# Layer norm statistics inside a state-space scan: ScalarE running sums in the place of VectorE batch-norm instructions

## The reference

```
def _layernorm(x, axis=-1, eps=1e-05):
    m = jnp.mean(x, axis=axis, keepdims=True)
    v = jnp.var(x, axis=axis, keepdims=True)
    return (x - m) / jnp.sqrt(v + eps)
...
    h = _layernorm(x, axis=-1) * (1 + ca) + sa
    x = x + ga * _L1_attn_ref(h, L1_attn_W_in, L1_attn_conv_w, L1_attn_conv_b, L1_attn_W_xproj, L1_attn_log_A, L1_attn_D_param, L1_attn_W_out)
    h = _layernorm(x, axis=-1) * (1 + cb) + sb
    x = x + gb * _L1_ffn_ref(h, L1_ffn_router_w, L1_ffn_w1, L1_ffn_w2, L1_ffn_bias)
```

## Time and profile before

| | us |
|---|---|
| median of 3 runs | 1818.52 (1814.84 to 1818.67) |
| the profiled execution, device time | 1820.8 |
| its span | 1819.1 |
| busy: PE, POOL, DVE, ACT over the whole span | 1502.0, 1346.1, 1152.2, 797.8 |
| stretch 1330 to 1602 (272 us): DVE busy | 258.09 |
| the same stretch: ACT, POOL, PE busy | 164.75, 194.84, 155.26 |
| mean granted TensorE clock, of full speed | 0.907 |

### The profile page before, as it was taken

One profiled execution on the slowest core, in us unless ns is written; L12 is line 12 of the kernel. 1 busy time (PEld: TensorE's weight loads), 2 busy tenths in 40 slices (PEclk: granted clock), 3 DMA queues, 4 the chain that ended last, 5 costly groups with the idle time before them and its releaser, 6 DMA issues. The chain is left out here.

```text
span 1819.1 us, 26796 instructions
## 1 busy us (share of the span) xinstructions
PE 1502.0 (83%) x8699; PEld 1034.9 (57%) x8699; DVE 1152.2 (63%) x2579; ACT 797.8 (44%) x1379; POOL 1346.1 (74%) x1154
## 2 busy tenths in 40 slices
PE   5899999999999999999999998988965664357970
PEld 3455556766556755656755657877833232136960
DVE  6866766566676575676566504755589998952224
ACT  2245444345444344444344453444486775323320
POOL 5587988788898698898788783536576657658376
PEclk7699999999999999999999998999977876667995
DMA  6333334231222122131131103024485555424333
GB/s 177 70 89 82 71 71 83 70 70 42 65 58 48 48 56 50 36 70 36 47 70 36 36 13 86 23 72 114 109 199 126 141 133 132 108 69 146 99 86 87
DMA packets 125761, 146.65 MB, mean 81 GB/s; under 512 B 15784, under 2 KB 84796, under 8 KB 125624
## 3 DMA queue, kind: packets, MB, share of 16 engines
q1 hardware_dynamic: 118456, 130.60, 29.3%
q0 software_dynamic: 7168, 14.34, 2.9%
HBM read 65.24 MB, written 29.42 MB: 52 GB/s over the span
## 5 line engine op out<-in xcount | busy, mean ns | idle before, releaser
L838 DVE CUSTOM_DVE_ANT_0 ring<-ring,mask 128x128 f32<-128x128 f32 (+7 forms) x512 | 383.8, 769 | 186.3 <-PE ring L700 185.9
L924 ACT ACTIVATE prob<-ring 128x512 f32<-128x512 f32 x576 | 315.2, 597 | 298.1 <-PE ring L715 294.5
L978 POOL TENSOR_TENSOR acc<-acc,prob 128x512 f32<-128x512 f32 x272 | 353.1, 1298 | 73.0 <-ACT prob L924 49.4
L731 PE MATMUL ps_o<-prob,v 128*64 128x256 f32 x2304 | 282.5, 387 | 3.9 <-issue 3.8
L700 PE MATMUL ring<-k,x 128*128 128x512 f32 (+3 forms) x768 | 252.0, 408 | 35.8 <-ACT prob L924 22.1
L714 PE MATMUL ring<-x,k 128*128 128x512 f32 x576 | 258.1, 448 | 24.6 <-DVE neg_m L838 15.4
L715 PE MATMUL ring<-x,k 128*128 128x512 f32 x576 | 229.4, 398 | 0.0
L700 PEld LDWEIGHTS ring<-k,x 128*128 128x128 f32 x768 | 137.3, 198 | 144.5 <-ACT prob L924 50.9
L731 PEld LDWEIGHTS ps_o<-prob,v 128*64 128x64 f32 x2304 | 154.6, 137 | 106.5 <-issue 39.6
L2929 POOL TENSOR_TENSOR m_hc<-m_st,m_crep 128x1024 f32<-128x1024 f32 x64 | 150.8, 2357 | 71.7 <-DVE m_st L2672 64.0
L975 POOL TENSOR_TENSOR acc<-prob 128x512 f32<-128x512 f32 x144 | 184.4, 1281 | 8.5 <-ACT prob L924 7.2
(11 more groups left out here) (414 smaller groups left out, 2816.1 us busy)
## 6 DMA issues: line engine op xcount, KB each, us to landing
x<-other SPq DMA_DIRECT2D x256, 128.0 KB, 2.3
m_x_rep<-u_mem SPq DMA_DIRECT2D x64, 512.0 KB, 4.7
x<-rot SPq DMA_DIRECT2D x128, 128.0 KB, 2.3
sorted_in<-zeros SPq DMA_DIRECT2D x3, 1548.0 KB, 11.9
e_sorted<-sorted_in SPq DMA_DIRECT2D x18, 258.0 KB, 3.7
sorted_out<-e_hid SPq DMA_DIRECT2D x18, 256.0 KB, 2.2
slots_in<-zeros SPq DMA_DIRECT2D x2, 2048.0 KB, 8.7
slots_out<-wo SPq DMA_DIRECT2D x16, 256.0 KB, 2.4
```

What stands on the lines that cost most here:

```text
L731: mm = e.matmul(ps_o[s * D:(s + 1) * D, qb % 2 * 2 * P:(qb % 2 + 1) * 2 * P], v[g % 2][:, kb, :], prob[i % NPROB][:, s * 2 * P:(s + 1) * 2 ...
L838: e.tensor_tensor_reduce(ps, ps, mask_1[:, SEQ - n:SEQ], 1.0, -3.0 * NEG, ALU.add, ALU.min, neg_m[g % 2][:, c, h, qb % QPC:qb % QPC + 1]). ...
L924: e.activation(prob[i % NPROB][:, :], banks(("s2",) + key, BANK), ACT.Exp, scale=-1.0).then_inc(s2_exp.sem, 1)
L978: e.tensor_tensor(total[:, :], total[:, :], tile[:, :], ALU.add).then_inc(summed.sem, 1)
```

## The change

For `join` and for `out` of batches 0 to 2 (ten halves in all), the statistics are made by ScalarE:

- the copy of a PSUM bank, one instruction of 128x512, becomes four of 128x128, each with a running sum over its row into `row_sum`;
- at the plan positions of `sums` and `stats`, ACT makes `row_mid` = -sum/128 (128x4) and then, behind a semaphore wait, four 128x128 squares of (x + row_mid), each with a running sum into `row_sq`; the squares themselves go to a scratch tile;
- at `rstd1` and `rstd3`, ACT makes the mean and the variance (two 128x8 copies into `mv`), and takes the logarithm with the scale 1/128 from `row_sq`.

DVE loses the ten calls of `row_stats`. The last batch's `out` keeps its statistics on DVE. The plan is the same.

```
+        row_sum, row_mid, row_sq, squares = sb("row_sum", (P, TILES)), sb("row_mid", (P, TILES)), sb("row_sq", (P, TILES)), sb("squares", (P, 4, HID))
...
+            elif kind == "sums" or kind == "stats" and key[0] < BATCH - 1:
+                act.add(step), act.add(step)
...
-                elif kind == "sums":
-                    b, n = key
-                    tile = b * TPB + 4 * n
-                    e.wait_ge(act.sem, act.at["join", b, n])
-                    row_stats(e, x, stats, mv, range(tile, tile + 4), row_chain)
-                    stats_at["sums", b] = row_chain.n
...
-                elif kind == "stats":
+                elif kind == "stats" and key[0] == BATCH - 1:
...
+        def copy_rows(e, bank, tile):
+
+            for j in range(4):
+                i = tile + j
+                t = e.activation(x[:, i, :], bank[:, j * HID:(j + 1) * HID], ACT.Copy, accum_out=row_sum[:, i:i + 1])
+            return t
+
+        def square_rows(e, tile, step, copied):
+
+            ts = slice(tile, tile + 4)
+            e.wait_ge(*copied)
+            e.activation(row_mid[:, ts], row_sum[:, ts], ACT.Copy, scale=-1.0 / HID).then_inc(act.sem, 1)
+            e.wait_ge(act.sem, act.at[step] - 1)
+            for i in range(tile, tile + 4):
+                t = e.activation(squares[:, i - tile, :], x[:, i, :], ACT.Square, bias=row_mid[:, i:i + 1], accum_out=row_sq[:, i:i + 1])
+            t.then_inc(act.sem, 1)
+
+        def row_moments(e, b, step):
+
+            ts = slice(b * TPB, (b + 1) * TPB)
+            e.wait_ge(act.sem, act.at[step])
+            e.activation(mv[:, ts, 0], row_sum[:, ts], ACT.Copy, scale=1.0 / HID)
+            e.activation(mv[:, ts, 1], row_sq[:, ts], ACT.Copy, scale=1.0 / HID)
+            return ts
...
-                    e.activation(x[:, tile:tile + 4, :], bank[:, :].rearrange("p (j n) -> p j n", n=HID), ACT.Copy).then_inc(act.sem, 1)
+                    copy_rows(e, bank, tile).then_inc(act.sem, 1)
+                elif kind == "sums":
+                    square_rows(e, key[0] * TPB + 4 * key[1], step, (act.sem, act.at[("join",) + key]))
+                elif kind == "stats" and key[0] < BATCH - 1:
+                    square_rows(e, key[0] * TPB + 4 * key[1], step, (add_act.sem, add_act.at[key]))
...
-                    e.wait_ge(row_chain.sem, stats_at["sums", b])
-                    e.activation(log_var[:, ts], mv[:, ts, 1], ACT.Ln, bias=eps[:, 0:1]).then_inc(rstd_act, 1)
+                    ts = row_moments(e, b, ("sums", b, 1))
+                    e.activation(log_var[:, ts], row_sq[:, ts], ACT.Ln, bias=eps[:, 0:1], scale=1.0 / HID).then_inc(rstd_act, 1)
...
-                    e.activation(x[:, tile:tile + 4, :], ps_w[turn[step] % NW][:, :].rearrange("p (j n) -> p j n", j=4),
-                                 ACT.Copy).then_inc(add_act.sem, 1)
+                    if b < BATCH - 1:
+                        copy_rows(e, ps_w[turn[step] % NW], tile).then_inc(add_act.sem, 1)
```

More of the change, by code:

```diff
@@ L2832, in scalar @@
                     b, = key
-                    ts = slice(b * TPB, (b + 1) * TPB)
-                    e.wait_ge(row_chain.sem, stats_at[b, 1])
-                    e.activation(log_var3[:, ts], mv[:, ts, 1], ACT.Ln, bias=eps[:, 0:1]).then_inc(rstd3_act, 1)
+                    if b < BATCH - 1:
+                        ts = row_moments(e, b, ("stats", b, 1))
+                        e.activation(log_var3[:, ts], row_sq[:, ts], ACT.Ln, bias=eps[:, 0:1], scale=1.0 / HID).then_inc(rstd3_act, 1)
+                    else:
+                        ts = slice(b * TPB, (b + 1) * TPB)
+                        e.wait_ge(row_chain.sem, stats_at[b, 1])
+                        e.activation(log_var3[:, ts], mv[:, ts, 1], ACT.Ln, bias=eps[:, 0:1]).then_inc(rstd3_act, 1)
                     e.wait_ge(rstd3_act, 2 * b + 1)
@@ L2871, in scalar @@
                     e.wait_ge(w_pe.sem, w_pe.at[step])
-                    e.activation(x[:, tile:tile + 4, :], ps_w[turn[step] % NW][:, :].rearrange("p (j n) -> p j n", j=4),
-                                 ACT.Copy).then_inc(add_act.sem, 1)
+                    if b < BATCH - 1:
+                        copy_rows(e, ps_w[turn[step] % NW], tile).then_inc(add_act.sem, 1)
+                    else:
+                        e.activation(x[:, tile:tile + 4, :], ps_w[turn[step] % NW][:, :].rearrange("p (j n) -> p j n", j=4),
+                                     ACT.Copy).then_inc(add_act.sem, 1)
                 elif kind == "raw":
```

1 line of the change is left out of this document (removed).

## The result

| | before | after |
|---|---|---|
| median, us (7 runs each, one chip) | 1818.24 | 1825.92 |
| lowest to highest, us | 1814.84 to 1822.28 | 1821.95 to 1828.91 |
| ratio of after to before, 95% interval | | 1.0042 [1.0029, 1.0055] |
| span of the profiled execution, us | 1819.1 | 1827.1 |

The change costs 7.7 us. The forecast was 16.5 us over the median then known (1835 against 1818.5) with a range of 1822 to 1846: the direction and the range hold, the size is more than twice too large.

What follows compares the result with a forecast made beforehand. The prediction held that DVE waits for ACT's chains at four places, where additions to ACT count: 5.5 + 5.9 + 4.6 + 3.3 - 2.4 = 16.9 us, so 1835 us from 1818.5, range 1822 to 1846.

Steps and rivals of the forecast that it cites:

- E: Batch-3 stretch, where DVE is the bound: two halves of statistics less gain in full, -2.4 us.
- A: Batch-0 stretch up to `late_delta`: the second `join` 2 copy and both sets of squares delay DVE, +5.5 us.
- B: From the second `join` 3 copy to `b_in` and batch 1's first product: copy and both squares exposed, +5.9 us.
- Rival (1): Whole scan: DVE stays the bound and ACT's additions run in idle time; faster, 1805 us, chance 0.09.
- The stall of the earlier trace: Batch-3 stretch: small DVE operation lasting 1.97 us until POOL's product ends; could shift 2 us to either side.
- r: What a running sum adds to one ACT instruction: taken as 0.20 us, bounds 0 and 0.30.
- c: Extra ACT time of a half copied in four pieces with sums: 0.31 + 4r, taken as 1.11 us.
- s: ACT time of the squares of a half, with `row_mid` and sums: 1.60 + 4r, taken as 2.40 us.
- C: Batch-1 stretch up to its `late_delta`: copies 0.9 and squares 4.8, less 1.1 of slack, +4.6 us.
- D: Batch-2 stretch: copies 0.9 and one set of squares 2.4 delay PE's counting and so DVE, +3.3 us.

Runs made afterwards that it cites:

- e3: Changed kernel with every set of four squares made a second time into buffers nobody reads; 1880.79 us, ratio 1.0129 to the kernel before.
- e2: Kernel before with only the `join` statistics moved to ACT, those of `out` staying on DVE; 1867.12 us, ratio 1.0044 to the kernel before.
- e1: Kernel before with only the `out` statistics of batches 0 to 2 moved to ACT, those of `join` staying on DVE; 1859.42 against 1858.21 us, ratio 1.0007.
- e7: Changed kernel with the same copies and squares but no running sums, constants in the sums' buffers; 1863.94 against 1866.42 us for the changed kernel.
- e6: Changed kernel, unedited, traced a second time on another chip; 1866.42 us, ratio 1.0045 to the kernel before.
- e9: Kernel before with only the copies in four pieces with unread running sums, all statistics on DVE; 1819.71 against 1819.48 us, ratio 1.0007.
- e4: Changed kernel with the squares and what follows from them moved behind `soft` in the plan; 1863.89 us, ratio 1.0022 to the kernel before.
- e10: Kernel before with only the statistics of batch 2's `out` moved to ACT; 1816.90 against 1819.48 us, ratio 0.9984.

## Why the prediction was right in kind and wrong in size

**What held.** What bounds the kernel was read rightly: DVE waits at four joints for ACT, and an addition to ACT ahead of them counts in full. The four waits grew, E gave its 2.2 us, and e3 shows A and B as pure ACT chains, in which all of an added 3.08 us is exposed, and e2 shows that they don't depend on the `out` part. Rival (1), by ACT's busy share, was off by more than 20 us. The stall of the earlier trace rows came back unchanged in the changed kernel, as DVE's timeline has it, so its term was zero there; that it can move is seen in e1 (2.85 us):

```profile
1558.27 1.97 DVE L1116 TENSOR_TENSOR f_less<-f_scores,f_best 128x64 f32<-128x64 f32 x1
```

**The term that failed first: r.** The prediction took 0.20 for a running sum, "since a read on ACT should be nearest to ACT's own shortest". The read's row does last that long, but its price is the distance between starts, 0.09. The rows that tell duration from price were there in the kernel before. ACT's timeline behind the first `late_delta`:

```profile
1369.77 0.21 ACT L2830 ACTIVATE m_rstd<-m_log_var 128x8 f32<-128x8 f32 x1
1369.88 1.13 ACT L2910 ACTIVATE m_da<-attn_t,m_a_neg 128x1024 f32<-128x1024 f32 x1
```

The operation of 0.21 us holds its engine for 0.11 where the next one doesn't wait for it. With r = 0.09 the prediction's own formulas (c = 0.67, s = 1.96) give 4.15 + 4.6 + 2.9 + 2.0 - 2.4 = 11.2 instead of 16.9: 5.7 us of the miss.

**The constants.** c and s came out at 0.53 and 1.78 where the formulas with r = 0.09 say 0.67 and 1.96: three more instructions of a split copy cost 0.18 and not 0.31, and `row_mid` is 0.23 ahead of the squares, not 0.33. With the measured values the sum is 3.65 + 4.1 + 2.67 + 1.8 - 2.4 = 9.8, another 1.4 us. By the figures in the Trainium skill ("ScalarE: Activation LUTs", section on what a table load costs) four squares without sums are, an estimate, near 1.3 us, and e7 agrees with 1.28.

**C.** With the measured prices C is 2 x 1.78 + 0.2 - 1.09 = 2.67: both squares, the two small copies of the moments of 0.10 each, the slack of `soft`, and nothing for the `out` copies, since the waits of 0.45 and 0.83 us are longer than what two copies add. At the low clock the runs have 2.7 (e3), at the clock of the profiled execution 0.4. The step that failed is the credit given to ACT's waits for PE: I counted on 0.45 and 0.83 us, and took 1.27, 1.09 and 1.10 us in the same stretch as fixed. They stay with a convolution of 5.9 us. In the profiled execution it took 3.59 us, and 2.65 us of these waits went, of which 0.37 came back ahead of the second `out` copy. These 2.3 us are the miss of C. Why the clock rose earlier there is open: the same kernel didn't repeat it (e6), and a part of the change in it isn't excluded.

**The rest.** B took up 0.33 more than forecast, mainly a wait of 0.23 before the second `z`, and A 0.2, for which a wait before `raw` went with 0.57 in place of 0.44. D was 0.1 less in this pair of traces (and 1.3 less in the second), E 0.16 less negative. So 16.9 - 5.7 - 1.4 - 2.3 - 0.33 - 0.2 - 0.1 + 0.16 = 7.0, the sum of A to E. The tail's 1.4 us, for which the prediction had no term, is the clock of PE in the last output projection: from the fold to the counting it takes 8.22 us against 6.82. e9, whose statistics are all on DVE, loses as much there, and e1 doesn't; what sets the clock there is open. The median, 7.7 us over before, lies between the sums without and with the tail (7.05 and 8.4).

**The range.** It was set by r from 0 to 0.30, and the result lies in its lower part. With r = 0 the prediction said 1826, and the median is 1825.9. That agreement is luck: r is 0.09, with which the prediction's own formulas give 1830, and most of the other 4 us are c and s, which came out cheaper still, and the waits of C.

## What to carry over

Price an added instruction by the distance from its start to the next one's in rows of the same engine, not by its duration: on ACT small rows of 0.2 us stand 0.10 apart. Before moving work from a full engine to one with room, look which engine ends the full one's waits at each joint; only the stretch where that is nobody (here the last, E) gains, and moving that part alone was the one version faster than the kernel before (0.9984 [0.9971, 0.9997], and 0.9990 [0.9971, 1.0010] on the other chip, which doesn't exclude no gain). Look as well who needs the result, and when: e4 put the squares where nobody waited behind them, and then their results came late. Give each such stretch its own distance between two fixed operations: A, B and E repeated within 0.01 us in the changed kernel, where its run times scatter over 7 us. Where such a distance holds an engine's waits for PE, give it two ends, one for each level of PE's clock: that was C and D here.

## What the runs showed of the hardware that I had not expected

- ACT's running sum: an ACTIVATION_READ_ACCUMULATOR row of 0.18 to 0.23 us behind each ACTIVATE, which adds 0.09 us (e7: 0.36 to 0.37 for four).
- Four ACTIVATEs of 128x128 from PSUM without a sum take 0.80 us up to the next instruction, one of 128x512 some 0.62: only 0.06 for each further instruction.
- The granted clock of PE at one and the same place of the program differs between traces, among those of one chip too (e9 and e10: 3.59 and 5.84 us, in two kernels that do the same there but for ACT's copies): the batch-1 convolution had 0.61, 1.00, 0.67 and 0.59 (before, after, e6, e3), 3.59 to 6.15 us for the same eight products. C of the changed kernel, which ACT's chain sets, differs by 1.1 us between its two traces for it; C of the kernel before and of e9, which DVE sets, stays within 0.02 us while the convolution goes from 3.59 to 6.15.
- A small DVE operation (128x64) lasts until POOL's product beside it ends, to 0.1 us: 1.36, 1.97, 2.40, 2.54 and 2.85 us for one and the same operation (e4, before, e3, e7, e1). The shortest row of this kind in the scan of the kernel before is 0.23.
